# Keys and values of a perceiver cross-attention: five float32r products over 128 rows in place of two fp32 products over 96 rows

## The reference, cut to what matters

```
q = (layernorm(x) @ Wq + bq)          # 128 x 256
k = (ctx @ Wk + bk)                   # 12544 x 256, contraction over 192
v = (ctx @ Wv + bv)                   # 12544 x 256, contraction over 192
attn = softmax(q k^T / 4)             # per head; the first layer clips the scores to +-10000
x = x + (attn v) @ Wo + bo
```

## Time and profile before

| | |
|---|---|
| median of three runs | 1392.23 us |
| the profiled execution | 1387.69 us, of which the span of the trace 1385.9 us |
| mean granted TensorE clock | 0.92 of full speed |
| PE / PEld busy | 88% / 57% of the span |
| DVE / ACT / POOL busy | 52% / 51% / 16% |
| L0's loop of attention | 68 to 550 us of the span |
| L1's loop of attention | 797 to 1278 us |

### The profile page before, as it was taken

The page is one execution under the profiler, slowest core; times in us unless marked ns, Lnnn a source line. Parts: engine busy times, 40 slices in busy tenths (PEclk is TensorE's granted clock), DMA queues, the critical chain, the costliest instruction groups (busy, mean ns, idle before and its releaser), DMA issues.

```text
span 1385.9 us, 29435 instructions
## 1 busy us (share of the span) xinstructions
PE 1216.7 (88%) x12725; PEld 784.6 (57%) x12725; DVE 716.0 (52%) x1348; ACT 712.6 (51%) x991; POOL 224.6 (16%) x118
## 2 busy tenths in 40 slices
PE   8799999999999988315899799999999999988556
PEld 6256666666666655315697256666566666555345
DVE  2546555555555563577222545555555555563431
ACT  3246666666666657152113256666666666657110
POOL 0222222222222200041000222222222222200000
PEclk9689999999999999558799799999999999999568
DMA  8969777777777660610706969777777777660803
GB/s 146 135 84 122 95 95 95 99 93 97 99 96 95 76 150 2 217 53 27 277 1 106 131 92 126 96 88 97 97 91 97 96 97 95 75 117 2 326 11 55
DMA packets 85155, 140.31 MB, mean 101 GB/s; under 512 B 9112, under 2 KB 76384, under 8 KB 84512
## 3 DMA queue, kind: packets, MB, share of 16 engines
q1 hardware_dynamic: 84128, 138.29, 63.9%
q10 hardware_dynamic: 896, 0.12, 0.1%
HBM read 60.05 MB, written 0.18 MB: 43 GB/s over the span
## 4 chain that ended last, share of the span: by engine, by line
PE 73%; DVE 16%; DMA 5%; issue 2%; ACT 2%; POOL 0%; SPq 0%; ACTq 0%; DVEq 0%; POOLq 0%
PE ring L547 40%; PE st L547 16%; PE ot L547 15%; DVE mpart L1202 8%; DMA qst<-rowb 3%; DVE arena L1329 2%; PE ring L678 1%; DMA arena<-scratch_perm 1%; DVE arena L1333 1%; ACT arena L921 1%; PE ring L553 0%; DMA warena<-ctxT 0%; PE ring L646 0%; DVE work L1323 0%; POOL arena L536 0%
## 5 line engine op out<-in xcount | busy, mean ns | idle before, releaser
L1202 DVE TENSOR_REDUCE mpart<-ring 128x1 f32<-128x448 f32 x896 | 516.7, 621 | 435.2 <-PE ring L547 432.8
L944 ACT ACTIVATE work<-st 128x1024 f32<-128x1024 f32 x392 | 400.8, 1022 | 197.7 <-PE st L547 193.1
L547 PE MATMUL ring<-arena,qst 96*128 96x448 bf16 x896 | 299.8, 369 | 4.9 <-DVE mpart L1202 2.7
L547 PE MATMUL st<-qst,arena 97*128 97x128 bf16 x3136 | 245.0, 221 | 19.5 <-DMA qst<-rowb 18.2
L547 PE MATMUL ot<-work,arena 128*17 128x128 f32 x6272 | 250.4, 277 | 8.9 <-issue 6.7
L547 PEld LDWEIGHTS st<-qst,arena 97*128 97x128 bf16 x3136 | 199.0, 99 | 84.3 <-issue 31.9
L547 PEld LDWEIGHTS ot<-work,arena 128*17 128x17 f32 x6272 | 138.5, 97 | 151.3 <-issue 103.7
L499 POOL TENSOR_TENSOR arena<-arena 128x896 f32<-128x896 f32 x52 | 98.2, 1888 | 715.6 <-ACT arena L917 715.6
L547 PE MATMUL ring<-warena,wkv 96*128 96x448 f32 x448 | 195.4, 566 | 2.0 <-DVE mpart L1202 1.3
L547 PE MATMUL ring<-wkv,warena 96*128 96x256 f32 x784 | 190.2, 385 | 0.9 <-DVE mpart L1202 0.8
L547 PEld LDWEIGHTS ring<-wkv,warena 96*128 96x128 f32 x784 | 147.4, 191 | 28.4 <-DVE mpart L1202 11.1
(11 more groups left out here) (269 smaller groups left out, 645.3 us busy)
## 6 DMA issues: line engine op xcount, KB each, us to landing
arena<-arena SPq DMA_DIRECT2D x336, 224.0 KB, 11.4
warena<-ctxT SPq DMA_DIRECT2D x28, 672.0 KB, 13.3
arena<-ffn_W SPq DMA_DIRECT2D x16, 1024.0 KB, 12.4
arena<-f SPq DMA_DIRECT2D x2, 4096.0 KB, 24.4
arena<-scratch_bc SPq DMA_DIRECT2D x1, 2048.0 KB, 6.7
arena<-scratch_perm SPq DMA_DIRECT2D x2, 1024.0 KB, 10.2
arena<-rows SPq DMA_DIRECT2D x1, 1792.0 KB, 7.0
warena<-w_in_proj SPq DMA_DIRECT2D x1, 1024.0 KB
```

The lines of the kernel that those rows point to most:

```text
L547: return nc.tensor.matmul(o, l, r, start=start, stop=stop, **kw)
L944: nc.scalar.activation(pbuf[:, n % 2], st[:, 2 * (n % 2):2 * (n % 2) + 2].rearrange("p b k -> p (b k)"), ACT.Exp).then_inc(*signal(f"{lay} ...
L1202: V.reduce_max(mpart[:, 2 * h + hf:2 * h + hf + 1], ring[:, BANKS[step][0], 0:HALF], AX_X).then_inc(*signal(f"{lay}_b_max"))
```

## The change

The 192 context features are now handled as 128 and 64. For each chunk the context is split into a high part, rounded to float32r, and the exact rest. Three tiles of 128 partitions hold them: `X_HI` and `X_LO` the parts of features 0 to 127, `X_MIX` the two parts of the last 64 features above each other. The weights are split in the same way into four tiles. Steps `k` and `v` use five float32r products of 128 rows: high by high, high by low, low by high, and the mixed tile by the high and by the low part of the last weights. PE's order, the tile sizes (448 columns for `k`, 256 for `v`) and the evictions stay.

The splits are new work: POOL splits the weights once per layer (two copies and two subtractions of 128x512), and the context of chunks 1 to 13 (`split_context`: two copies and a subtraction on 64 partitions, a copy and a subtraction on 128, all of 896 columns), ahead of `split(c)` in POOL's order. DVE splits the context of chunk 0, ahead of its work on the queries. PE waits for these splits in place of the loads. The context is loaded in three DMAs (128 rows, and the last 64 rows twice), the weights in three. Several semaphores are now shared by both layers (`of`), which adds no instruction to the path. The wide path of the first layer (`general_path`), which is not entered with these inputs, loads its own copy of the weights.

```diff
+X_HI, X_MIX, X_LO = range(3)
+W_HI, W_LO, W_TAIL_HI, W_TAIL_LO = range(4)
+PRODUCTS = ((X_HI, W_HI), (X_HI, W_LO), (X_LO, W_HI), (X_MIX, W_TAIL_HI), (X_MIX, W_TAIL_LO))
+CTX_LOADS, W_LOADS, CTX_STEPS = 3, 3, 5
+TAIL = CC - P
...
-                for n in range(2):
-                    load(wkv[:, :, n], a[f"{lay}_wkv"][n].rearrange("(k p) n -> p k n", p=CP), f"{lay}_wkv_in")
+                load(wkv[:, W_LO], a[f"{lay}_wkv"][:, 0:P].rearrange("n p d -> p n d"), f"{lay}_wkv_in")
+                for part in range(2):
+                    load(wkv[part * TAIL:(part + 1) * TAIL, W_TAIL_LO],
+                         a[f"{lay}_wkv"][:, P:CC].rearrange("n p d -> p n d"), f"{lay}_wkv_in")
...
-                load(ctxt[0:CP, par], a["ctxT"].rearrange("(k p) n -> p k n", p=CP)[:, :, bass.ds(at, CK)],
-                     f"{lay}_ctx_in{par}")
+                load(ctxt[:, par, X_LO], a["ctxT"][0:P, at:at + CK], f"{lay}_ctx_in{par}")
+                for part in range(2):
+                    load(ctxt[part * TAIL:(part + 1) * TAIL, par, X_MIX], a["ctxT"][P:CC, at:at + CK],
+                         f"{lay}_ctx_in{par}")
...
+                def split_context(c):
+                    raw, x = ctxt[:, c % 2], ctxr[:, c % 2]
+                    tail = slice(TAIL, P)
+                    pool.wait_ge(sem(f"{lay}_ctx_in{c % 2}"), 16 * CTX_LOADS * (c // 2 + 1))
+                    context(nc.gpsimd.tensor_copy(x[0:TAIL, X_MIX], raw[0:TAIL, X_MIX]), False)
+                    context(nc.gpsimd.tensor_copy(x[tail, X_HI], raw[tail, X_MIX]))
+                    context(nc.gpsimd.tensor_tensor(x[tail, X_MIX], raw[tail, X_MIX],
+                                                    x[tail, X_HI].bitcast(F32), ALU.subtract))
+                    context(nc.gpsimd.tensor_copy(x[:, X_HI], raw[:, X_LO]))
+                    context(nc.gpsimd.tensor_tensor(x[:, X_LO], raw[:, X_LO], x[:, X_HI].bitcast(F32), ALU.subtract))
+
+                def split_weights():
+                    pool.wait_ge(sem(f"{lay}_wkv_in"), 16 * W_LOADS)
+                    for n, (hi, lo) in enumerate(((W_HI, W_LO), (W_TAIL_HI, W_TAIL_LO))):
+                        nc.gpsimd.tensor_copy(wkvr[:, hi], wkv[:, lo]).then_inc(sem(f"{lay}_w_split"), 1)
+                        pool.wait_ge(sem(f"{lay}_w_split"), 2 * n + 1)
+                        nc.gpsimd.tensor_tensor(wkvr[:, lo], wkv[:, lo], wkvr[:, hi].bitcast(F32), ALU.subtract
+                                                ).then_inc(sem(f"{lay}_w_split"), 1)
+                    pool.wait_ge(sem(f"{lay}_w_split"), 4)
...
                 pool.wait_ge(sem(f"{lay}_ones_set"), 2)
+                split_weights()
+                split_context(1)
                 split(1)
...
                 for c in range(2, NCH):
+                    split_context(c)
                     split(c)
...
-                pe.wait_ge(sem(f"{lay}_wkv_in"), 32)
+                pe.wait_ge(sem(f"{lay}_w_split"), 4)
...
                     if kind == "k":
                         m, hf = n // 2, n % 2
-                        if n == 0:
-                            pe.wait_ge(sem(f"{lay}_ctx_in{c % 2}"), 16 * (c // 2 + 1))
-                        project(ring[:, bank, 0:HALF], lambda k: wkv[:, k, 0, m * P:(m + 1) * P],
-                                lambda k: ctxt[0:CP, c % 2, k, hf * HALF:(hf + 1) * HALF], f"{lay}_k_full", 2)
+                        if (c, n) == (0, 0):
+                            pe.wait_ge(sem(f"{lay}_x_first"), CTX_STEPS)
+                        elif n == 0:
+                            pe.wait_ge(sem(f"{lay}_x_split"), CTX_STEPS * c)
+                        project(ring[:, bank, 0:HALF], lambda k: wkvr[:, PRODUCTS[k][1], 0, m * P:(m + 1) * P],
+                                lambda k: ctxr[:, c % 2, PRODUCTS[k][0], hf * HALF:(hf + 1) * HALF],
+                                "k_full", len(PRODUCTS))
                     if kind == "v":
                         for t in range(2 * n, min(2 * n + 2, TPC)):
                             last = project(ring[:, bank, (t % 2) * D:(t % 2 + 1) * D],
-                                           lambda k: ctxt[0:CP, c % 2, k, t * P:(t + 1) * P],
-                                           lambda k: wkv[:, k, 1, :], None, 2)
+                                           lambda k: ctxr[:, c % 2, PRODUCTS[k][0], t * P:(t + 1) * P],
+                                           lambda k: wkvr[:, PRODUCTS[k][1], 1], None, len(PRODUCTS))
...
             def attention(lay, bq, bv, bo):
                 norm(f"{lay}_ln", xr[:, :], xn[:, :])
 
+                raw, x, tail = ctxt[:, 0], ctxr[:, 0], slice(TAIL, P)
+                dve.wait_ge(sem(f"{lay}_ctx_in0"), 16 * CTX_LOADS)
+                V.tensor_copy(x[0:TAIL, X_MIX], raw[0:TAIL, X_MIX]).then_inc(sem(f"{lay}_x_first"), 1)
...
+                V.tensor_tensor(x[:, X_LO], raw[:, X_LO], x[:, X_HI].bitcast(F32), ALU.subtract
+                                ).then_inc(sem(f"{lay}_x_first"), 1)
+
                 q = tmp[1].rearrange("p (k t) -> p k t", k=KC)
```

More of the change, by code:

```diff
@@ L25 @@
 I32 = mybir.dt.int32
+F32R = mybir.dt.float32r
 AX_X = mybir.AxisListType.X
@@ L362, in build @@
                                        ("vsum", (D + 1,)), ("avg", (P,)), ("one", (P,)), ("m", (H,)),
-                                       ("oT", (H, VW)), ("use", (D,)), ("keep", (D,)), ("mean", (D,))))
+                                       ("oT", (H, VW)), ("use", (D,)), ("keep", (D,)), ("mean", (D,)),
+                                                       ("wk", (2, D)), ("wv", (2, D))))
         pdiag = af(20480, ES * NG).rearrange("p (e g) -> p e g", g=NG)
@@ L445, in _ @@
             with sp.If(is_wild > 0):
+                for n, name in enumerate(("wk", "wv")):
+                    load(g_[name][0:CP], a["L0_wkv"][n].rearrange("(k p) n -> p k n", p=CP), "g_wkv_in")
                 with sp.Fori(0, TILES) as t:
@@ L509, in third, with context @@
-                    pool.wait_ge(sem(f"{lay}_k3_done"), KC * c + m + 1)
+                                            ).then_inc(*signal("k3_done"))
+                    pool.wait_ge(*of(lay, "k3_done", KC * c + m + 1))
+                count = [0]
+                def context(ins, then=True):
+                    count[0] += 1
+                    ins.then_inc(sem(f"{lay}_x_split"), 1)
+                    if then:
+                        pool.wait_ge(sem(f"{lay}_x_split"), count[0])
+                def split_context(c):
[8 more added lines that the diff above has]
+                    context(nc.gpsimd.tensor_tensor(x[:, X_LO], raw[:, X_LO], x[:, X_HI].bitcast(F32), ALU.subtract))
@@ L580, in general_path @@
                     last.then_inc(sem("g_mb_full"), 1)
+                    pe.wait_ge(sem("g_wkv_in"), 32)
                     with pe.Fori(0, TILES) as t:
@@ L644, in attention @@
                     if kind == "row":
-                        pe.wait_ge(sem(f"{lay}_m_done"), c + 1)
-                        nc.tensor.transpose(ring[0:H, bank, 0:TOK], nmf[:, c % 2], ident).then_inc(*signal(f"{lay}_row_full"))
+                        pe.wait_ge(*of(lay, "m_done", c + 1))
+                        nc.tensor.transpose(ring[0:H, bank, 0:TOK], nmf[:, c % 2], ident).then_inc(*signal("row_full"))
                     if kind == "s":
@@ L678, in attention @@
                             last = nc.tensor.transpose(ring[:, bank, g * P:(g + 1) * P], ots[:, g * P:(g + 1) * P], ident)
-                        last.then_inc(*signal(f"{lay}_o_full"))
+                        last.then_inc(*signal("o_full"))
                 if lay == "L0":
@@ L938, in attention @@
                         act.dma_start(qst[CP:CP + 1, c % 2], rowb[:, :]).then_inc(sem(f"{lay}_row_in"), 16)
-                        nc.scalar.activation(alpha[:, c % 2], mdiff[:, :], ACT.Exp).then_inc(*signal(f"{lay}_alpha_done"))
+                        nc.scalar.activation(alpha[:, c % 2], mdiff[:, :], ACT.Exp).then_inc(*signal("alpha_done"))
                     if kind == "e":
@@ L1166, in attention @@
                 norm(f"{lay}_ln", xr[:, :], xn[:, :])
+                raw, x, tail = ctxt[:, 0], ctxr[:, 0], slice(TAIL, P)
+                dve.wait_ge(sem(f"{lay}_ctx_in0"), 16 * CTX_LOADS)
+                V.tensor_copy(x[0:TAIL, X_MIX], raw[0:TAIL, X_MIX]).then_inc(sem(f"{lay}_x_first"), 1)
+                V.tensor_copy(x[tail, X_HI], raw[tail, X_MIX]).then_inc(sem(f"{lay}_x_first"), 1)
+                dve.wait_ge(sem(f"{lay}_x_first"), 2)
+                V.tensor_tensor(x[tail, X_MIX], raw[tail, X_MIX], x[tail, X_HI].bitcast(F32), ALU.subtract
+                                ).then_inc(sem(f"{lay}_x_first"), 1)
+                dve.wait_ge(sem(f"{lay}_x_first"), 3)
+                V.tensor_copy(x[:, X_HI], raw[:, X_LO]).then_inc(sem(f"{lay}_x_first"), 1)
+                dve.wait_ge(sem(f"{lay}_x_first"), 4)
+                V.tensor_tensor(x[:, X_LO], raw[:, X_LO], x[:, X_HI].bitcast(F32), ALU.subtract
```

(1 more changed line is left out.)

80 lines of the change are left out of this document (44 added, 36 removed).

## The result

The changed kernel takes 1403.94 us in the median of 20 runs (1387.73 to 1412.64), the kernel before 1392.03 in 20 runs beside it (1386.18 to 1394.81): a ratio of 1.0074, 95% interval 1.0056 to 1.0091. The ratio is of the runs within 1.5% of the fastest, 16 of the 20 (median 1402.0 us), and the profiled execution, 1412.64 us (span 1410.9; before 1387.69, span 1385.9), is one of the other four. I had forecast 1327, with a range of 1283 to 1375, and given 0.85 to faster. It became slower by 0.7%, outside the range. I read shares and patterns from the trace and compare times by the ratios to the kernel before.

A forecast was written before the change was run, and what follows sets the result against it. PE was taken to bound the attention loops. Product gains, layer starts, the k(3,0) wait and ACT summed as -101 + 9.7 + 20.6 + 5.5 = -65: 1322.5 us for the profiled execution, 1327 for the median, range 1283 to 1375.

The forecast's parts named there:

- Step 2: Both layers' loops: 11.25 chunks of k and 12 of v gain per layer, 50.5 us each, 101 for both.
- step 1: PE's k and v products: 5 passes instead of 8, gaining 2.2 us per chunk for k and 2.15 for v.
- step 5: ACT and DMAs in the loop: some ACT work surfaces, 0.25 us per chunk, 5.5 in all; DMA backlog hidden.
- rival D: In the loop the row DMA falls into the DMA backlog, a chunk loses 1 to 2 us: 1360; chance 0.06.
- Step 3: Start of each layer: context bytes and splits delay the loop's first s, L0 +3 us, L1 +6.7 us.
- Step 4: Ahead of k(3,0): PE waits 7.8 us for POOL's context split, then half clock; 10.3 us per layer, 20.6 in all.
- The lock: DVE and POOL exclude each other, so L0's splits run in turn: start 1 to 3 us later, median 1328 to 1330.
- A: Steps k and v: a float32r product takes as long as a record of before; slower, 1490 us; chance 0.13.
- B: Layer starts and k(3,0): the waits are covered, since PE comes late to them; 1291 us; chance 0.12.
- C: POOL's split takes 12 us or more; PE stands about 1 us in 20 chunks, 5 more in chunk 3: 1357; chance 0.10.

The follow-up runs named there:

- a_paced6: Changed kernel; from chunk 2 on SP waits before the 7th of a chunk's 12 stack transfers until those issued have landed: 1340.9 us, ratio 0.9641.
- a_hoist: Changed kernel with chunk 3's context split put ahead of the rest of chunk 2's keys on POOL, no SP wait added: 1388.7 us, ratio 0.9978.
- a_paced6_late_hoist: Changed kernel with SP's wait before the 7th stack transfer from chunk 3 on, and chunk 3's split ahead of chunk 2's remaining keys on POOL: 1327.5 us.

## Why the prediction was wrong

**What failed** is the sentence under the views: "inside the loops time taken from PE's list of steps is time taken from the kernel, as long as the next engine, ACT, keeps up". Step 2 multiplied the gain of step 1 by the chunks on its strength, and step 5 looked only at ACT and at the DMAs' own data. PE's instructions come by DMA as well, late behind a burst of the stack, and that supply was already at its limit before (the two pauses there, behind counts of 444 and 469). The forecast kernel, with that limit moved by one wait, exists: it takes 1340.9 us. The limit itself cost some 60 us.

The profiled executions say where the forecast was lost. From POOL's first subtraction of chunk 3 to that of chunk 13, ten periods in each layer, they took 722.3 us before and 720.4 after: 1.8 us gained where the forecast has 20 x 4.2 = 84. Everything outside these periods cost 26.8 us more than before, where the forecast leaves 19. In `a_paced6` the same two numbers are 70.1 gained and 21.0 paid. The changed kernel has 46.9 us more of pauses than the kernel before and 110 us more at half clock, which costs up to half its length; `a_paced6` still has 49 of these 110 (273 us), so not all of them belong to the pauses.

**The clue stood in the trace of before.** The timeline of PE, before:

```profile
498.83 0.82 PE L547 MATMUL ot<-work,arena 128*17 128x128 f32 x9 [3.38 <-issue]
```

There was another of 3.35 us at 1227.69. I read PE's waits by their sums, where 6.7 us are small, and didn't ask what these two were. No rival had this mechanism; rival D (0.06) had the DMAs' backlog, but for the row's transfer.

Point by point:

- **Step 1, right, a little too large.** v's products are (4.36 - 0.28)/34 = 0.120 us apart, forecast 0.111; k's (4.18 - 0.37)/19 = 0.200 in twenty at full clock of `a_paced6` (a median of 0.205 in the loop after), forecast 0.190. The gain is 3.8 us per chunk instead of 4.35. That row of `a_paced6`:

```profile
736.88 4.18 PE L608 MATMUL ring<-ctxr,wkvr 128*128 128x448 f32 x20
```

  The groups of the two products after, whose means hold the half clock:

```profile
L605 PE MATMUL ring<-ctxr,wkvr 128*128 128x448 f32 x560 | 171.9, 451 | 38.5 <-POOL ctxr L554 24.2
...
L605 PE MATMUL ring<-wkvr,ctxr 128*128 128x256 f32 x980 | 150.4, 299 | 8.6 <-ACT arena L990 4.2
```

- **Step 2, wrong as it was put, mostly right without the pauses.** With the pauses gone a chunk takes 32.8 us, 3.2 less than before. Step 1 was short by 0.55 us per chunk, which is half of the 1.1 to the forecast 31.7.
- **Step 3, right in kind, too small.** The first s of L0 stands at 73.71, +5.8 us (forecast +3). SP issues the first contexts of L1 at 747.53 (before 736.12), and the first s comes at 816.95, 69.4 us later; before 61.0: +8.4 (forecast +6.7). A term that I had not put is POOL's split of chunk 2's contexts: the first k(2,0) of L1 waited 4.89 us for it.
- **Step 4, right, its worth too high.** Forecast 7.8 us, measured 8.77; a split of 7.2 us, forecast 6.6. The rows of POOL's operations on `ctxr`, duration min/median/max in ns:

```profile
L553 POOL CAST ctxr<-warena x26: 931/932/1011, 22.0 to 1199.9; 128x896 fp32r<-128x896 f32 x26
L554 POOL TENSOR_TENSOR ctxr<-warena,ctxr x26: 2070/2103/2125, 23.0 to 1201.0; 128x896 fp32r<-128x896 f32 x26
```

  The copies cost 0.93 and not 0.83, the subtractions 2.10 and not 1.89. Taken away it is worth 13 us (`a_hoist`) or 14 (`a_paced6_late_hoist`), I had put 20.6. In later chunks the split was hidden, as forecast.
- **Step 5, wrong in what it looked for.** ACT was not the bound (70 of 100 us busy in the window of `a_paced6`). Of the 3.8 us of step 1 a chunk gave back 3.2 there, so 0.6 surfaced somewhere, where I had put 0.25. The DMAs' data were hidden; what their backlog does to PE's instructions was not.
- **The lock.** It is in the trace after: in L1 a subtraction of 128 x 256 on DVE took 2.31 us at 760.69, beside POOL's from 760.59 to 762.72; in the kernel before, with POOL at rest, it took 0.43 (742.65). By the rule of the Trainium skill, "SBUF — State Buffer", section "SBUF: two separate sides", the two exclude each other; the trace agrees. In L0 DVE's last subtraction of the context and the four operations of the queries' split took 4.58 us beside POOL, for 2.53 alone: 2.0 us on DVE, where I had put 1 to 3. But the splits did not run one after the other, since POOL's weights came only at 12.64, when DVE's split was nearly done.
- **Rivals.** A is out: a product of 256 columns takes 0.120 us, not 0.216. (Its threshold was reckoned wrong: the gain falls to 0.36 of itself where a product takes 1.36 times its one pass, not 1.5.) B is out, the waits are there. C's 12 us are 7.2. D is out: the row's waits were 18.1 us in all, before 18.2.

What stays open: why a block's transfer starts so late. The experiments show that it does while 12 stack transfers are out and less so with 6, 4 or 2; they don't show where it is held. The one pause left in `a_paced6` (1.9 us at 477.19) was not looked into. A better spread than one wait before the 7th was not searched for.

## What to carry to other kernels

A pause of PE that the profile puts down to "issue" in the middle of an unrolled list is worth a look even if there are only two: PE may be out of instructions, because its blocks wait behind a burst of data transfers. Such pauses lie whole blocks apart in PE's list, whatever step they fall into. Before PE's instructions are made shorter or more numerous, count how many of them start between two of the instruction queue's transfers; here near 500 there was no room left, and behind a block that was late itself PE stopped after 350 to 400. Bursts on a data queue should be broken up, by no more than is needed, since the small transfers that others wait for can come late by it.

## What the runs showed that I had not expected

- PE never started more than 517 records between the starts of two instruction transfers in the loops, in any of the 17 kernels, and all 22 pauses of the changed kernel end 1.4 to 2.0 us after such a transfer has landed.
- One wait of SP, for transfers that it doesn't need itself, was worth some 60 us of 1402, with the same bytes and more of them per us (107 to 116 GB/s in the window from 200 to 300).
- Such a pause can cost more than its length: behind 17 of the 22 the granted clock fell to half. Behind the one of 2.46 us the step k at 142.86 ran at half clock and took 2.31 us; behind the one of 1.83 us the step at 251.57 ran at full clock and took 1.35.
